# Layer 0's tail on ScalarE: each front modulated at the head of a step, the second absolute sum behind all modulations

## The reference, cut to what matters

```
h   = gamma * layernorm(x) + beta          # gamma, beta from the condition
q, k, v = h @ Wqkv.T + bqkv
out = softmax(q k^T) v / sqrt(512) @ Wp.T + bp
h1  = out + x
x1  = (gamma * layernorm(h1) + beta) + h1
```

## Time and profile before

| what | value |
|---|---|
| median of 3 runs | 2775.66 us (2775.62 to 2777.38) |
| the profiled execution, its own time | 2772.19 us |
| its span | 2770.4 us |
| TensorE busy | 2607.1 us (94%) |
| VectorE busy | 2149.7 us (78%) |
| ScalarE busy | 1841.1 us (66%) |
| GpSimd busy | 1963.1 us (71%) |
| TensorE's granted clock, mean | 0.984 |
| DMA moved | 260.42 MB, mean 94 GB/s |

### The profile page before, as it was taken

How to read it: one execution, slowest core, us unless ns; L and a number is a source line. 1 busy time by engine, 2 the same in 40 slices (tenths; PEclk the granted TensorE clock), 3 DMA queues, 4 the chain that set the end, 5 groups by cost and what they waited for, 6 DMA issues and landing times. The chain is left out here.

```text
span 2770.4 us, 59968 instructions
## 1 busy us (share of the span) xinstructions
PE 2607.1 (94%) x21716; PEld 1458.3 (53%) x21761; DVE 2149.7 (78%) x4440; ACT 1841.1 (66%) x3320; POOL 1963.1 (71%) x1579
## 2 busy tenths in 40 slices
PE   7899999999999999999769998999899999987997
PEld 5655566555665547555335554555455445543443
DVE  5777778776787768877667778777877787768997
ACT  4366665666566675566556677667766776667996
POOL 0298844897359872789749887987789778965542
PEclk9999999999999999999989999999999999999999
DMA  6122353224432335223223214321332232245444
GB/s 236 39 59 59 113 169 108 59 59 150 143 96 61 88 111 173 72 58 101 85 73 82 59 33 119 82 59 29 110 82 59 46 106 59 59 164 182 104 103 110
DMA packets 168764, 260.42 MB, mean 94 GB/s; under 512 B 85388, under 2 KB 91668, under 8 KB 167576
## 3 DMA queue, kind: packets, MB, share of 16 engines
q1 hardware_dynamic: 166680, 250.27, 33.0%
q0 software_dynamic: 1792, 6.33, 0.6%
HBM read 99.15 MB, written 38.88 MB: 50 GB/s over the span
## 5 line engine op out<-in xcount | busy, mean ns | idle before, releaser
L547 DVE TENSOR_REDUCE a_mxs<-ps 128x1 f32<-128x512 f32 x2048 | 1267.8, 680 | 258.8 <-PE ps L414 256.2
L508 ACT ACTIVATE a_p<-ps 128x512 f32<-128x512 f32 x2048 | 1043.6, 605 | 203.3 <-PE ps L428 193.1
L368 POOL TENSOR_TENSOR a_sum<-a_p 128x512 f32<-128x512 f32 x736 | 940.0, 1287 | 201.8 <-PE ps L448 112.8
L414 PE MATMUL ps<-a_k,a_q 96*128 96x512 f32 x2048 | 854.6, 424 | 25.8 <-DVE a_mxs L547 20.8
L428 PE MATMUL ps<-a_q,a_k 98*128 98x512 f32 x2048 | 807.3, 419 | 15.6 <-ACT a_p L508 9.8
L448 PE MATMUL ps<-a_sum,a_unit 128*32 128x512 f32 x1536 | 650.5, 596 | 0.6 <-POOL a_sum L368 0.6
L374 POOL TENSOR_TENSOR a_sum<-a_sum,a_p 128x512 f32<-128x512 f32 x480 | 619.3, 1290 | 37.6
L448 PE MATMUL ps<-a_p,xv 128*32 128x512 f32 x3968 | 638.9, 595 | 0.0
L414 PEld LDWEIGHTS ps<-a_k,a_q 96*128 96x128 f32 x2048 | 388.7, 190 | 258.5 <-DVE a_mxs L547 104.9
L428 PEld LDWEIGHTS ps<-a_q,a_k 98*128 98x128 f32 x2048 | 383.9, 189 | 243.3 <-ACT a_p L508 144.9
L517 ACT ACTIVATE a_ots<-ps 128x512 f32<-128x512 f32 x256 | 152.8, 598 | 402.7 <-PE ps L448 401.6
(11 more groups left out here) (253 smaller groups left out, 3080.6 us busy)
## 6 DMA issues: line engine op xcount, KB each, us to landing
a_q<-qh SPq DMA_DIRECT2D x256, 128.0 KB, 2.3
a_k<-kh SPq DMA_DIRECT2D x256, 128.0 KB, 2.4
a_q<-ql SPq DMA_DIRECT2D x128, 128.0 KB, 2.3
a_k<-kl SPq DMA_DIRECT2D x128, 128.0 KB, 2.4
x<-a_p SPq DMA_DIRECT2D x64, 256.0 KB, 2.2
a_p<-in_w_fc SPq DMA_DIRECT2D x12, 1024.0 KB, 7.9
kh<-in_x SPq DMA_DIRECT2D x4, 2048.0 KB, 14.5
a_p<-x SPq DMA_DIRECT2D x16, 512.0 KB, 5.8
```

Source lines behind the costliest of these rows:

```text
L368: pair = pool.tensor_tensor(tile, keys[0], keys[1], ALU.add)
L414: pe.matmul(self.mx[self.mx_ring[at]], self.q[j][0:96, t * P:(t + 1) * P], self.k[j][0:96, half * HALF:(half + 1) * HALF], start=True, sto ...
L508: act.activation(self.key_tile(u, kt), self.st[self.st_ring[CHUNKS * k + n]], ACT.Exp, scale=self.scale).then_inc(self.s_exp, 1)
L547: dve.reduce_max(self.mxs[:, k % 2, c:c + 1], self.mx[self.mx_ring[CHUNKS * k + c]], axis=AX.X).then_inc(self.s_mxr, 1)
```

## The change

In steps t >= 3 of a tail that is not the last, ScalarE modulates front t - 3 at the head of the step, ahead of the normalization of tile t - 1; before, it modulated front t - 4 at the end of steps t >= 4. Behind the loop fronts 6 and 7 remain. Front 5 is no longer in `EXACT`: ScalarE makes both of its values. VectorE's `rest` of front t - 4 comes at step t instead of t - 6. The first absolute sum stays in step 3; the second moves from the end of step 5 to the place behind all modulations.

```
-        EXACT = lambda b: (5, 7) if b else (4, 5, 6, 7)
-        exacts = lambda b, n: 4 * min(b, 1) + 2 * max(b - 1, 0) + sum(i < n for i in EXACT(b))
+        EXACT = lambda b: (7,) if b else (4, 5, 6, 7)
+        exacts = lambda b, n: 4 * min(b, 1) + max(b - 1, 0) + sum(i < n for i in EXACT(b))
...
                             normalize(2 * t + 1)
+                        if not last and 3 <= t:
+                            modulate(b + 1, (t - 3,))
                         if 1 <= t <= TT:
...
                             if not last:
-                                act.wait_ge(s_wsum, done(b + 1) + (t - 2) // 2)
+                                act.wait_ge(s_wsum, done(b + 1) + min(1, (t - 2) // 2))
                             square(b, t - 3)
...
-                        if not last and 4 <= t:
-                            modulate(b + 1, (t - 4,))
-                        if not last and t in (3, 5):
+                        if not last and t == 3:
                             act.wait_ge(s_ss, TT * b + t - 2 + 1)
-                            absolute(b + 1, (t - 3) // 2)
+                            absolute(b + 1, 0)
                     if not last:
-                        modulate(b + 1, range(5, UN))
+                        modulate(b + 1, range(6, UN))
+                        act.wait_ge(s_ss, TT * b + TT - 3 + 1)
+                        absolute(b + 1, 1)
                         act.wait_ge(s_wsum, done(b + 1) + 2)
...
-                        if t >= 6 and not last:
-                            rest(b + 1, t - 6)
+                        if t >= 4 and not last:
+                            rest(b + 1, t - 4)
...
                     if not last:
-                        for n in EXACT(b + 1):
-                            exact(b + 1, n)
-                        for n in range(4, UN):
+                        exact(b + 1, 7)
+                        for n in (6, 7):
                             rest(b + 1, n)
```

## The result

| | before | after |
|---|---|---|
| median of the runs (lowest to highest), us | 2776.03 (2774.42 to 2777.54, n = 6) | 2797.13 (2795.64 to 2801.98, n = 6) |
| ratio, 95% interval | | 1.0079 [1.0069, 1.0090] |
| profiled span, us | 2770.4 | 2798.7 |
| mean granted clock of TensorE | 0.984 | 0.976 |

The kernel became slower by 21.1 us. The forecast was 2787.4, with a range of 2778 to 2793: the direction held, and the time lies 4.1 us above the range.

The account below looks back on a forecast made before the run. Two walls per tail bound it: ScalarE's modulation, and the chain of multiplications, shift and load before unit 12. Late stores cost three tails 3.9 us each, 11.7 onto 2775.66: 2787.4 us, own range 2783 to 2792, overall 2778 to 2793.

Parts of the forecast that it names:

- part 3: SyncE's queue: two loads and eight stores take 13.2 us from issue, so stores land at 727.5, 11 us later.
- Part 1: Earlier modulations remove TensorE's stops of 1.50 and 0.57 us at unit 0; TensorE is 2.5 us ahead by unit 2.
- Part 2: Second absolute sum starts at 712.3; SyncE's second loads leave at 714.3, 11.7 us later, with eight x1 stores behind them.
- Part 4: VectorE waits for the stores; its eighth multiplication and unit 12 come 3.9 us later per tail, unit 12 at 750.0.
- unit 7's wait: Unit 7, due at 726.2, starts at about 728.2, waiting for unit 3's `s_lo`; costs nothing more.
- The sum: Three tails at 3.9 us each add 11.7 us (9.0 to 14.7), for a median of 2787.4 us.
- The stores pass the loads: Rival, 12%: stores served ahead of SyncE's two loads land at 722.3; 1.3 us earlier per tail, 2771.8 us.
- The second wall moves forward with the first: Rival, 7%: unheld by stores, VectorE's multiplications, shift and load before unit 12 come 2.5 us earlier per tail; 2768.2 us.
- The tail's own steps become late: Rival, 13%: ScalarE's waits at step heads make the last step 1 us late; 3 us more, 2790.4 us.
- The page of the Trainium skill: HBM side limits transfers to about 358 GB/s; stores land 1.1 us later, 3.4 us more in all; not in the forecast.

Follow-up runs that it names:

- run 2: The change with its second absolute sum put back at the end of step 5, leaving the modulations alone; 2772.23 us, 0.9990 of the kernel before.
- Run 4: The change with 16 unused matmuls into a free bank ahead of unit 12's wait; 2792.31 us, 1.0065 of the kernel before.
- run 6: The change with the second sum between modulations of fronts 5 and 6, and five stores, the loads, three stores on SyncE; 2772.86 us, ratio 0.9991.
- run 8: The change with the second sum at the end of step 5 and three unused matmuls ahead of the last fronts; 2772.12 us, ratio 0.9984.
- run 5: The change with the eight stores ahead of the second loads and 12 unused matmuls ahead of unit 12's wait; 2780.06 us, ratio 1.0015.
- run 7: The change with its second absolute sum at the end of step 4; 2773.72 us, 0.9998 of the kernel before.
- run 1: The change with SyncE's eight stores of x1 ahead of the wait for the second sum and the two loads; 2781.71 us, ratio 1.0026.
- run 3: The kernel before with only its second absolute sum moved behind all modulations; 2802.84 us, ratio 1.0101.

## Why the prediction was right and wrong

Two steps failed. The first is a term that the sum lacked: the slow unit behind the longer stop at unit 12, put at nothing, measured 6.4 us over the three tails. The second is the landing in part 3, put at 13.2 us and measured at 14.2 to 15.7, worth 4.5 us. The path (late sum, late loads, late stores, VectorE, unit 12) was right.

**Part 1, right.** Forecast for the middle tail: unit 0 at 706.9, unit 2 at 712.4. Measured 713.61 - 6.98 = 706.6 and 719.42 - 6.98 = 712.4. That the gain drowns at unit 12 was right as well; run 2 shows what it is where it doesn't drown: 2 us in tail 1, and about nothing in the others.

**Part 2, right.** Sum at 712.3, issue at 714.3: measured 719.27 - 6.98 = 712.29 and 721.28 - 6.98 = 714.30, the stores behind it.

**Part 3, right in kind, mis-sized.** "13.2 us" from issue to landing was 14.2, 15.7 and 14.2 (VectorE's resumption behind the issue, 394.25 - 380.07, 736.96 - 721.28, 1078.89 - 1064.70), at and above my upper end of 14.2. My lower bound had 10.6 us of data at 397 GB/s and 1.7 us for start and completion together. In the middle tail the start alone took 1.7 us (721.28 to 723), a dip to some 240 GB/s for 2 us cost 0.8 more, and the last 2 us are 35 KB; by 735.0, 13.7 us behind the issue, all else was through. All three bursts have the dip (242 and 277 GB/s in 386 to 388, 262 and 254 in 1069.7 to 1071.7), and the burst before had it as well, where I read only the full stretch behind it (windows, kernel before):
```profile
708.60:709.60 1.00, 1.00 (x5) 0.82 (x5) 1.00 (x2) 1.00 (x2) 0.00 (x0) 1.00 0.92 246
```
What makes the dip, and the middle tail's late last 35 KB, is not shown.

**Part 4, right in kind.** From VectorE's resumption to the eighth multiplication's end it is 743.84 + 1.39 - 736.96 = 8.27 us (forecast 8.3), and from there to unit 12 it is 759.40 - 745.23 = 14.17 (forecast 750.0 - 735.8 = 14.2). Unit 12 was late by 5.5, 6.3 and 5.3 us in its own tail and not by 3.9: 17.1 us in place of 11.7. Part 3's excess over 13.2 (1.0 + 2.5 + 1.0 = 4.5 us) is most of these 5.4. The rest, 0.9 us, lies mostly in tail 1, where the load of high weights took 4.64 us from its issue to unit 12 (412.90 to 417.54) and 3.95 in the middle tail.

**The sum lacked a term.** From unit 12 to the landmark it took 17.12 to 17.14 us before and 18.61, 19.62 and 19.59 after: +1.5, +2.5, +2.5, **6.4 us** of matmuls at the 1.2 GHz level; in tail 1 the clock was back within the unit (0.85 in 420.5 to 421.5). Run 4 takes 5.6 us of it away by filling the stops. I had named the stop ("after some 4 us or more of waiting on it") and priced only its length. I had dismissed unit 7's wait as free; it also fell to half clock (737.77, 1.70), and that was indeed absorbed by the wait at unit 12. Together: 11.7 + 5.4 + 6.4 = 23.5 us, the landmark's shift in the profiled executions; the medians differ by 21.1, and where the 2.4 us between them lie can't be said, since the other executions left no trace.

**The rivals.** *The stores pass the loads*: fell, they landed last. *The second wall moves forward with the first* (faster): fell for the change, but it is what runs 2 and 6 do, and with a gain of 2 to 3 us, not 7.5. *The tail's own steps become late*: fell, the fronts' wait is 1.26 to 1.27 us as before; but run 2 shows it for a sum that stays in step 5 while the modulations move up (1.90 to 2.17 us). The page of the Trainium skill that I weighed ("DMA: Bandwidth & Descriptors", Where 436 GB/s comes from) would have added 3.4 us. The trace does not agree with its rate of about 358 GB/s as a limit: 385 to 414 GB/s flow in each us from 729 to 734, and 410 in 759 to 760. That the mean over 722 to 733 is 326 comes from the start and the dip. Taken as a mean for the burst the page's figure would have sized the landing better, but by luck.

## What to carry to other kernels

When a step that releases a queue's next transfers is moved, price everything behind it in that queue on both sides: putting the other transfers first only moves the wait to another engine. Where a stop of TensorE gets longer, add the slow unit behind it (here 1.5 to 2.5 us) to the stop's length. Filling a stop with matmuls pays only where they end before the wait does: in run 8 the filling cost about what it won, in run 5 it held unit 12 back. Compare times in two traces from a point in the same tail, since the losses of the tails before add up. Size a burst by when its last transfer completes, not by when most of its bytes are through.

## What the runs showed of the hardware

The stop's length alone does not say whether the clock falls. After 1.26 us of idling ahead of the fronts TensorE went on at full clock (before, and after), after 1.90 and 2.17 us in run 2 unit 0 ran at half clock in tails 2 and 3, but after 1.90 us in tail 1 and after 2.14 in run 7 it did not. What distinguishes these is open: I made no run for it. The kernel after shows the same at unit 7. In tail 1 a stop of 0.65 us and then one of 1.23 were followed by 1.00, in tail 3 one of 0.68 us and then one of 1.17 by 0.50 (TensorE's timeline):
```profile
395.05 1.21 PE L1044 MATMUL ps<-a_h_hi,a_k 128*128 128x512 f32 x4 [1.23 <-DVE kl L1429]
...
1079.69 2.08 PE L1044 MATMUL ps<-a_h_hi,a_k 128*128 128x512 f32 x4 [1.17 <-DVE kl L1429]
```
At unit 12, 2.92 us of idling (run 1, middle tail), 3.64 (run 3) and 3.69 (the change) were each followed by a clock of 0.50. Sixteen matmuls with no use, 3.81 us, were enough to keep it at 1.00 there.

A burst of two loads of 1 MB and eight stores of 256 KB does not flow at one rate: in all three tails of the change it has a start of some 1.7 us, some 400 GB/s, a dip to 221 to 277 GB/s for about 2 us, and 400 GB/s again.
